# ScalarE one group ahead, VectorE copying the turned nodes, and products a group sooner, at the end of a graph layer

## The chip, the cores and the metric

The kernel runs on 1 core of one Trainium2 chip. The metric is the device time of a whole execution in microseconds. The engines are TensorE (PE, with its weight loads as PEld), VectorE (DVE), ScalarE (ACT), GpSimd (POOL) and SyncE (SP), each with its own instruction stream; they meet at semaphores. Everything is float32 where this case is concerned.

## What is computed

A graph of 6250 nodes with 128 features and 206250 edges goes through three graph convolutions, a layer norm, one attention layer and another layer norm. The change lies in the convolutions:

```
def _conv(x, row, col, edge_type, edge_weight, W, b):
    deg_inv_sqrt = jnp.where(deg > 0, deg ** (-0.5), 0)
    norm = deg_inv_sqrt[row] * deg_inv_sqrt[col] * edge_weight
    xw = jnp.einsum('ni,tio->tno', x, W)          # four edge types
    x_j = xw[edge_type, col] * norm[:, None]
    out = jax.ops.segment_sum(x_j, row, num_segments=N) + b
    return jax.nn.leaky_relu(out, negative_slope=0.01)
z1 = _conv(x, row, col, edge_type, edge_attr, W1, b1)
z2 = _conv(z1, row, col, edge_type, edge_attr, W2, b2)
z3 = _conv(z2, row, col, edge_type, edge_attr, W3, b3)
return (x + z1 + z2 + z3) / 4
```

## The kernel before

**Sizes.** Nodes are held as 49 blocks of 128 (`NB`), one node to a partition. The edges have been sorted by the block of their target row beforehand, into 1612 tiles of 128 edges. For each layer a table in memory (`gcn_table`) holds, for every node, its four products with the layer's four weight matrices, scaled by the node's `inv_deg`.

**A layer.** POOL issues one indirect transfer per tile (L718), which gathers the 128 table rows of the tile's edges into a ring of 93 tiles, `g_rows`. The other engines walk over 465 *groups* of four steps (`GRP`, `GP = 4`). A step is one tile and one target block; where a block begins inside a tile, the tile is used by two steps. In a group q:
- ACT (`scale_rows`, `scale`, L866 to L877) loads five registers from the list `gcn_at` (four ring slots and the last tile, L866), waits until the tile has landed (`s_land`) and copies four tiles with each edge's weight as scale to `g_step` (L877), a ring of three groups.
- DVE (`layer_gcn`) has built `g_hot` two groups before (L1579), four one-hot matrices in a ring of three.
- PE (`sum_gcn`, `add_up`, L1169 to L1180) loads four registers from `gcn_at`, zeroes a bank with one product (L1175) and adds four products of `g_hot` and `g_step` (L1180; each is two passes in the trace, so eight).
- DVE adds the bank to `acc` (L1588).

The first groups are in a hardware loop; the last ones are written out, with no loop.

**The end of a layer.** The first of the 49 blocks is sure to be complete at group 451 (`DONE_FROM`), and four more at each of the next 12 groups (`BATCHES`: one block, then twelve batches of four; `NBATCH = 13`). n is the batch, so group 451 + n. Of layers 0 and 1 each batch makes four blocks of the next layer's table:
- `next_z` on DVE (L1604, L1606, L1608): z of the batch, three instructions one after another, in the group n itself, behind the add to `acc`; then `s_z` is raised.
- `turn` on PE (L1141): four transposes of z into bank 4. In before they are put in group n + 1, as its last work.
- `turn` on ACT (L839): the copy of bank 4 to `nodeT`. It is a single buffer.
- `products` on PE (L1149): four products, nodeT of a block by the layer's 128x512 weights, into three banks in turn, so the fourth waits until the rows of the first are out. In before they are put in group n + 2, between the sums and the transposes.
- `rows_of` on ACT (L846): four copies to `rows` with `inv_deg` as scale, as the products come; SP writes each to the table (L492), through a ring of four.

So in before ACT's stream in group 451 + n is: registers, scale the group's own four tiles, rows of batch n - 2, copy of the turned batch n - 1. Before group 464 stand the rest: products 11, turn 12, products 12. POOL begins the next layer's gathers when all 49 table writes have landed and all of the layer's `g_rows` have been scaled (`s_copied`, all 465 groups).

Order is set by the code alone, since every engine's stream is written out by hand with its waits.

## Time and profile before

| | us |
|---|---|
| time before, median of 3 runs | 9099.33 (9099.24 to 9101.07) |
| the profiled execution's own time | 9109.24 |
| its span, first to last instruction | 9107.4 |
| PE busy | 5676.2 (62%) |
| DVE busy | 4601.6 (51%) |
| ACT busy | 3980.5 (44%) |
| POOL busy | 6423.1 (71%) |

The profiled execution is 9.9 us longer than the median. The busy shares are means over stages with different limits: sorting up to about 700 us, three layers up to about 6937 us, then attention. A line such as L718 is one source line of the kernel; "idle before" is what the engine stood still ahead of a group of instructions, and the arrow names what released it.

### The profile page before, as it was taken

What the parts mean: (1) busy time and instruction counts of PE and PEld (TensorE: products, weight loads), DVE (VectorE), ACT (ScalarE), POOL (GpSimd) and SP (SyncE); (2) the same over time, 40 slices, a digit from 0 to 9 for tenths busy, and PEclk for the clock granted to TensorE, in tenths of its full rate; (3) what the DMA queues carried; (4) which work ended last, traced back from release to release, by engine and by line L of the source; (5) the groups of instructions that cost most, each with busy time, mean ns of one, the idle gap of its engine ahead of it and who ended that gap; (6) DMA issues with size and microseconds to landing.
All of it is one profiled execution on the core that took longest, in us unless ns stands there. A gap on an engine that the chain in (4) does not pass through costs nothing.

```text
span 9107.4 us, 149340 instructions
## 1 busy us (share of the span) xinstructions
PE 5676.2 (62%) x32763; PEld 4294.9 (47%) x32764; DVE 4601.6 (51%) x12830; ACT 3980.5 (44%) x12251; POOL 6423.1 (71%) x6527
## 2 busy tenths in 40 slices
PE   4885555555555555555556555555654777777775
PEld 3664444444443444444443444444443666666665
DVE  9994232323233232322323232232325999999998
ACT  5552232323233232322323232232324888888887
POOL 0566777777775777777775777777775777777775
PEclk9996555555556555555556555555555787777876
DMA  1001111111123111111112111111111434343333
GB/s 50 32 35 54 53 53 53 53 53 53 53 67 79 53 53 53 53 53 53 53 53 90 53 53 53 53 53 53 53 53 57 117 114 116 115 115 115 115 115 94
DMA packets 432675, 612.43 MB, mean 67 GB/s; under 512 B 232026, under 2 KB 249479, under 8 KB 432527
## 3 DMA queue, kind: packets, MB, share of 16 engines
q0 software_dynamic: 208832, 428.96, 16.9%
q1 hardware_dynamic: 223694, 182.02, 6.3%
q14 instruction: 121, 0.98, 0.0%
q8 instruction: 28, 0.46, 0.0%
HBM read 437.29 MB, written 51.28 MB: 54 GB/s over the span
## 4 chain that ended last, share of the span: by engine, by line
issue 26%; POOL 25%; DMA 23%; DVE 18%; DVEq 4%; PE 4%; ACT 1%; POOLq 0%; ACTq 0%; SPq 0%
POOL g_rows L718 24%; DMA g_rows<-gcn_table,rec_idx 22%; DVEq L1563 3%; DVE a_miss L1674 2%; DVE a_max L1679 1%; DVE state L1732 1%; DVE lo_hot L1249 1%; DVE a_lo L1758 1%; DVE acc L1738 1%; DVE v_hot L1389 1%; PE wide L1149 1%; DVE a_sum L1702 1%; DVE state L1692 1%; DVE a_drop L1720 1%; DVE a_left L1753 1%
## 5 line engine op out<-in xcount | busy, mean ns | idle before, releaser
L718 POOL DMA_INDIRECT g_rows<-gcn_table,rec_idx x4836 | 4592.4, 950 | 1644.4 <-issue 1212.7
L877 ACT ACTIVATE g_step<-g_rows,rec_w 128x128 f32 x5580 | 1781.3, 389 | 4211.5 <-POOLq L698 3921.5
L1180 PE MATMUL bank<-g_step,g_hot 128*128 128x128 f32 x7440 | 1853.4, 428 | 1646.8 <-ACT g_step L877 1533.0
L1180 PEld LDWEIGHTS bank<-g_step,g_hot 128*128 128x128 f32 x7440 | 1593.5, 316 | 2078.9 <-issue 2078.9
L1588 DVE TENSOR_TENSOR acc<-acc,bank 128x512 f32 x930 | 639.9, 688 | 2765.4 <-PE bank L1180 2761.5
L743 POOL DMA_INDIRECT a_roll<-gat_table,src_plane x1612 | 1527.0, 947 | 494.4 <-issue 444.9
L1180 PE MATMUL wide<-g_step,g_hot 128*128 128x128 f32 x3720 | 930.0, 429 | 896.9 <-ACT g_step L877 871.0
L1180 PEld LDWEIGHTS wide<-g_step,g_hot 128*128 128x128 f32 x3720 | 799.8, 317 | 1111.7 <-issue 1111.7
L930 ACT ACTIVATE a_cand<-a_miss,a_rows 128x128 f32<-128x128 bf16 x3608 | 1096.0, 386 | 19.7 <-DMA a_rows<-a_roll 19.5
L1588 DVE TENSOR_TENSOR acc<-acc,wide 128x512 f32 x465 | 320.0, 688 | 1495.8 <-PE wide L1180 1494.1
L1579 DVE TENSOR_TENSOR g_hot<-bank,rec_lo 128x512 f32<-128x512 f32 x1395 | 952.7, 683 | 3.6 <-DVE z L1608 0.3
L1209 PE MATMUL bank<-a_msg,a_hot 128*128 128x130 f32 x3608 | 668.3, 341 | 384.8 <-DVE a_msg L1725 381.3
L1209 PEld LDWEIGHTS bank<-a_msg,a_hot 128*128 128x128 f32 x3608 | 566.7, 238 | 522.1 <-DVE a_msg L1725 402.3
L1200 PE MATMUL wide<-ident,a_cand 128*128 128x128 f32 x3608 | 689.1, 354 | 165.4 <-ACT a_cand L930 164.2
L1200 PEld LDWEIGHTS wide<-ident,a_cand 128*128 128x128 f32 x3608 | 551.8, 183 | 193.3 <-ACT a_cand L930 161.7
L580 POOL DMA_INDIRECT gcn_slots<-run,at_u x52 | 286.0, 5500 | 408.7 <-issue 399.0
L1679 DVE TENSOR_REDUCE a_max<-wide 128x2 f32<-128x1024 f32 x451 | 550.1, 1220 | 38.9 <-issue 24.9
L1175 PE MATMUL bank<-zeros 1*128 1x512 bf16 x930 | 537.1, 578 | 25.1 <-issue 8.1
L923 ACT ACTIVATE a_hot<-a_miss 128x512 f32<-128x512 bf16 x451 | 283.9, 629 | 255.2 <-DVE a_miss L1674 253.2
L1674 DVE TENSOR_TENSOR a_miss<-bank,a_lo 128x256 bf16<-128x256 f32 x902 | 375.8, 417 | 6.8 <-issue 0.8
L1725 DVE SCALAR_TENSOR_TENSOR a_msg<-bank,a_rows 128x520 f32<-128x520 f32 x451 | 312.5, 693 | 1.8 <-ACT bank L942 1.8
L918 ACT ACTIVATE a_hotT<-wide 128x512 bf16<-128x512 f32 x451 | 269.1, 597 | 87.1 <-DVE a_max L1679 77.5
(262 smaller groups left out, 5070.9 us busy)
## 6 DMA issues: line engine op xcount, KB each, us to landing
a_rows<-a_roll SPq DMA_DIRECT2D x451, 264.0 KB
g_rows<-gcn_table,rec_idx POOLq DMA_INDIRECT x4836
gcn_table<-rows SPq DMA_DIRECT2D x147, 256.0 KB, 2.0
a_roll<-gat_table,src_plane POOLq DMA_INDIRECT x1612
e_dst<-by_dst_dst SPq DMA_DIRECT2D x451, 2.0 KB
gat_table<-acc SPq DMA_DIRECT2D x7, 462.0 KB
out_x<-xs SPq DMA_DIRECT2D x6, 448.0 KB
gcn_slots<-nothing SPq DMA_DIRECT2D x4, 468.0 KB, 5.7
```

The source lines that it names most:

```text
L718: pool.indirect_dma_start(out=g_rows[:, tile % RING, :], out_offset=None, in_=gcn_tables[layer % 2], in_offset=bass.IndirectOffsetOnAxis(a ...
L743: pool.indirect_dma_start(out=a_roll[:, g % ROLL, t, :], out_offset=None, in_=gat_table, in_offset=bass.IndirectOffsetOnAxis(ap=src_plane[ ...
L877: last = nc.scalar.activation(g_step[:, j, k, :].unsqueeze(1), g_rows[:, bass.ds(slots[k], 1), :], ACT.Copy, scale=rec_w[:, bass.ds(q.at(0 ...
L930: last = nc.scalar.activation(a_cand[:, w, h, t, :], a_miss[:, j, t, :], ACT.Identity, scale=-BIG, bias=a_rows[:, j, t, ROW - HEADS + h:RO ...
L1175: nc.tensor.matmul(sums_of(j)[:, :], zeros[0:1, 0:1].to_broadcast([1, P]), zeros[0:1, 0:1].to_broadcast([1, GP * D]), start=True, stop=False)
L1180: last = nc.tensor.matmul(sums_of(j)[:, bass.ds(places[k], D)], g_hot[:, j % 3, k, :], g_step[:, j % 3, k, :], start=False, stop=(k == GP ...
L1200: last = nc.tensor.transpose(wide[:, w, h, t, :], a_cand[:, w, h, t, :], ident[:, :])
L1209: last = nc.tensor.matmul(pv_ps(j), a_hot[:, j, t, :], a_msg[:, j, t, :], start=(t == 0), stop=(t == T - 1))
L1579: V.tensor_tensor(g_hot[:, j, :, :], spread(iota_ps.unsqueeze(1), [P, GP, P]), spread(lo.unsqueeze(2), [P, GP, P]), ALU.is_equal).then_inc ...
L1588: V.tensor_tensor(dst_ap, dst_ap, sums_of(j).rearrange("p (k d) -> p k d", k=GP), ALU.add).then_inc(s_gadd, 1)
L1674: return V.tensor_tensor(a_miss[:, h, ts, :], spread(iota_ps.unsqueeze(1), [P, 2, P]), spread(a_lo[:, h, ts].unsqueeze(2), [P, 2, P]), ALU ...
L1679: V.tensor_reduce(a_max[:, m, :], wide[:, m % 2, :, :, :].rearrange("p h t e -> p h (t e)"), AX.X, ALU.max).then_inc(sa["max"], 1)
```

## The change

In the groups 451 to 463 of layers 0 and 1:
- ACT scales the tiles of the *following* group (group 451 does its own and the next), ahead of the rows; the registers for the group after that are loaded behind those copies (`slots_of`, kept in `ahead`). The rows come one batch sooner by number: those of n - 1 in group 451 + n.
- PE does the transposes of batch n at the end of the group 451 + n itself, and the products of batch n - 1 behind the sums; the registers of the next group are loaded between the products and the transposes.
- The copy of bank 4 to `nodeT` is DVE's, behind the batch's three z instructions, with a wait for the transposes. ACT has no such copy left.
- Before group 464 only the products and rows of batch 12 stand.

```
--- before.py
+++ after.py
@@ -832,12 +832,7 @@
             act.wait_ge(s_count, 9)

             def scale_rows(layer):
-                def turn(n):
-
-                    act.wait_ge(s_tT, turns(layer + 1, n) + 1)
-                    width = len(BATCHES[n])
-                    nc.scalar.copy(nodeT[:, 0:width, :].rearrange("p b e -> p (b e)"), bank[4][:, 0:width * P]
-                                   ).then_inc(s_tc, 1)
+                ahead = []

                 def rows_of(n):
                     for b in BATCHES[n]:
@@ -850,23 +845,26 @@
                     if not q.live(0):
                         return
                     n = q.base - DONE_FROM if q.i is None and layer < 2 else -1
-                    if n == NBATCH:
-                        rows_of(n - 2)
-                        turn(n - 1)
+                    if n <= 0:
+                        scale(q, slots_of(q))
+                    if 0 <= n < NBATCH:
+                        following = Step(GRP, q.base + 1)
+                        scale(following, ahead.pop() if n else slots_of(following))
+                        if n + 1 < NBATCH:
+                            ahead.append(slots_of(Step(GRP, q.base + 2)))
+                    if n >= 1:
                         rows_of(n - 1)
-                    scale(q)
-                    if 0 <= n < NBATCH:
-                        if n >= 2:
-                            rows_of(n - 2)
-                        if n >= 1:
-                            turn(n - 1)
-
-                def scale(q):
-                    j = q.slot(0) % 3
-                    _, (*found, tile) = nc.values_load_multi_w_load_instructions(
+
+                def slots_of(q):
+                    _, values = nc.values_load_multi_w_load_instructions(
                         gcn_at[32:33, bass.ds(q.at(0), 1), :].rearrange("p g k -> p (g k)"),
                         engines=(mybir.EngineType.Activation,), min_val=0, max_val=CH * CCOLS - 1,
                         skip_runtime_bounds_check_because="a step less the begun blocks, at most the last tile")
+                    return values
+
+                def scale(q, values):
+                    j = q.slot(0) % 3
+                    *found, tile = values
                     slots = [nc.s_assert_within(v, 0, RING - 1,
                                                 skip_runtime_bounds_check_because="a tile modulo the ring")
                              for v in found]
@@ -1132,6 +1130,8 @@
                     last.then_inc(s_flip, 1)

             def sum_gcn(layer):
+                ahead = []
+
                 def turn(n):

                     pe.wait_ge(s_z[layer + 1], BATCHES[n].stop)
@@ -1154,22 +1154,23 @@
                         return
                     n = q.base - DONE_FROM if q.i is None and layer < 2 else -1
                     if n == NBATCH:
-                        products(n - 2)
-                        turn(n - 1)
                         products(n - 1)
-                    add_up(q)
+                    add_up(q, ahead.pop() if n >= 1 else places_of(q))
                     if 0 <= n < NBATCH:
-                        if n >= 2:
-                            products(n - 2)
                         if n >= 1:
-                            turn(n - 1)
-
-                def add_up(q):
-                    j = q.slot(0)
+                            products(n - 1)
+                        ahead.append(places_of(Step(GRP, q.base + 1)))
+                        turn(n)
+
+                def places_of(q):
                     _, places = nc.values_load_multi_w_load_instructions(
                         gcn_at[64:65, bass.ds(q.at(0), 1), 0:GP].rearrange("p g k -> p (g k)"),
                         engines=(mybir.EngineType.PE,), min_val=0, max_val=(GP - 1) * D,
                         skip_runtime_bounds_check_because="a block less its group's first, at most one per step")
+                    return places
+
+                def add_up(q, places):
+                    j = q.slot(0)
                     if q.live(-3) or layer:
                         pe.wait_ge(s_gadd, q.at(-3, 1, ADDS * layer + 2))
                     nc.tensor.matmul(sums_of(j)[:, :], zeros[0:1, 0:1].to_broadcast([1, P]),
@@ -1591,6 +1592,11 @@
                         if 0 <= n < NBATCH:
                             dve.wait_ge(s_gadd, q.at(0, 1, adds + 2))
                             next_z(layer, slice(BATCHES[n].start, BATCHES[n].stop))
+                            if layer < 2:
+                                dve.wait_ge(s_tT, turns(layer + 1, n) + 1)
+                                width = len(BATCHES[n])
+                                V.tensor_copy(nodeT[:, 0:width, :].rearrange("p b e -> p (b e)"),
+                                              bank[4][:, 0:width * P]).then_inc(s_tc, 1)
                 run_steps(dve, GRP, 3, 2, body, NBATCH + 1)
                 dve.wait_ge(s_gadd, adds + ADDS)
```

PE's stream, one group of the written-out end of layer 0 (group 458, batch 7). L1149 are the products, L1141 the transposes, L1175 (in after L1176) the zeroing, L1180 (L1181) the sums. Before:

```order
L1149 MATMUL wide<-w_all,nodeT 128x512 [waits s_tr,s_tc]
L1149 MATMUL wide<-w_all,nodeT 128x512 [waits s_tr]
L1149 MATMUL bank<-w_all,nodeT 128x512 [waits s_tr]
L1149 MATMUL wide<-w_all,nodeT 128x512 [waits s_tr]
L1141 MATMUL wide<-ident,z 128x128 [waits s_tc,s_z1]
L1141 MATMUL wide<-ident,z 128x128 x3
L1169 TENSOR_LOAD gcn_at
L1175 MATMUL wide<-zeros 128x512 [waits s_gadd]
L1180 ISA [waits s_copied,s_ghot]
L1180 MATMUL wide<-g_step,g_hot 128x128
```

And after:

```order
L1149 MATMUL wide<-w_all,nodeT 128x512 [waits s_tr,s_tc]
L1149 MATMUL bank<-w_all,nodeT 128x512 [waits s_tr]
L1149 MATMUL wide<-w_all,nodeT 128x512 [waits s_tr] x2
L1166 TENSOR_LOAD gcn_at
L1141 MATMUL wide<-ident,z 128x128 [waits s_tc,s_z1]
L1141 MATMUL wide<-ident,z 128x128 x3
L1176 MATMUL wide<-zeros 128x512 [waits s_gadd]
L1181 ISA [waits s_copied,s_ghot]
L1181 MATMUL wide<-g_step,g_hot 128x128
```

The kinds of work stand in the same row, but the register load moved ahead of the transposes, and by the numbers of the batches the transposes are now those of the group's own batch, and the products those of the batch before it.

ACT's stream at the same place, from the scaling of one group to the next. L877 (in after L875) is one tile's scaling, L846 (L841) one block's rows, L839 the copy to nodeT, and the TENSOR_LOAD the five registers. Before:

```order
L866 TENSOR_LOAD gcn_at
L875 REGISTER_ALU [waits s_gpe]
L877 ISA [waits s_land]
L877 ACTIVATE g_step<-g_rows,rec_w 128x128
...
L846 ACTIVATE rows<-wide,inv_deg 128x512 [waits s_tw1,s_tm]
L846 ACTIVATE rows<-wide,inv_deg 128x512 [waits s_tw2,s_tm]
L846 ACTIVATE rows<-bank,inv_deg 128x512 [waits s_tw3,s_tm]
L846 ACTIVATE rows<-wide,inv_deg 128x512 [waits s_tw0,s_tm]
L839 COPY nodeT<-wide 128x512 [waits s_tT]
```

And after:

```order
L873 REGISTER_ALU [waits s_gpe]
L875 ISA [waits s_land]
L875 ACTIVATE g_step<-g_rows,rec_w 128x128
...
L859 TENSOR_LOAD gcn_at
L841 ACTIVATE rows<-wide,inv_deg 128x512 [waits s_tw1,s_tm]
L841 ACTIVATE rows<-wide,inv_deg 128x512 [waits s_tw2,s_tm]
L841 ACTIVATE rows<-bank,inv_deg 128x512 [waits s_tw3,s_tm]
L841 ACTIVATE rows<-wide,inv_deg 128x512 [waits s_tw0,s_tm]
```

The copy L839 left the stream, and the register load went from ahead of the scaling to behind it.

DVE's stream at the same place, in after, where L1589 is the add to acc, L1610 to L1614 the three z instructions and L1580 the one-hots of the group after next:

```order
L1589 TENSOR_TENSOR acc<-acc,wide 128x4x128
L1610 TENSOR_TENSOR z<-acc,inv_deg 128x512 [waits s_gadd]
L1612 TENSOR_TENSOR z<-z,bias 128x512 [waits s_chain]
L1614 SCALAR_TENSOR_TENSOR z<-z 128x512 [waits s_chain]
L1598 COPY nodeT<-wide 128x512 [waits s_chain,s_tT]
L1580 TENSOR_TENSOR g_hot<-bank,rec_lo 128x512 [waits s_gpe]
```

L1598 is the copy that came from ACT; before, the one-hots followed z at once.

## Rows read from the trace of the kernel before

**Rows 1.** Page: a group's instructions, busy us, mean ns, idle before it
```profile
L718 POOL DMA_INDIRECT g_rows<-gcn_table,rec_idx x4836 | 4592.4, 950 | 1644.4 <-issue 1212.7
```
**Rows 2.** Timeline of POOL at the boundaries: start us, us, and idle before
```profile
2736.13 1.15 POOL L718 DMA_INDIRECT g_rows<-gcn_table,rec_idx  x1 [0.30 <-issue]
2812.79 0.94 POOL L718 DMA_INDIRECT g_rows<-gcn_table,rec_idx  x1 [75.52 <-DMA gcn_table<-rows]
...
4911.65 0.94 POOL L718 DMA_INDIRECT g_rows<-gcn_table,rec_idx  x1 [77.64 <-DMA gcn_table<-rows]
```
**Rows 3.** Chain that ended last, the group from 2781 us: start, us, what
```profile
2782.78 1.15 PE bank L1180 x8
2783.93 1.52 PE bank L1149 x2
2785.45 2.76 PE wide L1149 x4
2788.20 0.87 PE bank L1149 x2
2789.10 0.69 ACT rows L846
2789.79 0.48 ACTq L866
2790.26 1.13 issue
```
**Rows 4.** Timeline of DVE, PE and ACT, a z hand-over, then the same group
```profile
2706.89 0.69 DVE L1608 SCALAR_TENSOR_TENSOR z<-z 128x512 f32<-128x512 f32 x1
...
2707.93 0.14 PEld L1141 LDWEIGHTS wide<-ident,z 128*128 128x128 f32 x1 [0.24 <-DVEq L1611]
...
2781.26 1.28 ACT L877 ACTIVATE g_step<-g_rows,rec_w 128x128 f32 x4 [1.31 <-issue]
...
2784.08 0.69 DVE L1588 TENSOR_TENSOR acc<-acc,bank 128x512 f32 x1 [6.61 <-PE bank L1180]
...
2786.25 0.69 DVE L1608 SCALAR_TENSOR_TENSOR z<-z 128x512 f32<-128x512 f32 x1
...
2788.47 0.14 PEld L1141 LDWEIGHTS wide<-ident,z 128*128 128x128 f32 x1 [0.24 <-issue]
...
2789.43 0.38 PE L1175 MATMUL bank<-zeros 1*128 1x512 bf16 x1
2789.69 0.58 ACT L839 COPY nodeT<-wide 128x512 f32<-128x512 f32 x1
2791.56 1.28 ACT L877 ACTIVATE g_step<-g_rows,rec_w 128x128 f32 x4 [1.30 <-issue]
```
**Rows 5.** Timeline, the last batch's products (before group 464)
```profile
2805.60 0.30 PEld L1149 LDWEIGHTS bank<-w_all,nodeT 128*128 128x128 f32 x2 [1.06 <-ACT nodeT L839]
...
2809.23 0.09 PEld L1175 LDWEIGHTS wide<-zeros 1*128 1x128 bf16 x1 [0.76 <-issue]
...
2809.34 0.69 ACT L846 ACTIVATE rows<-bank,inv_deg 128x512 f32<-128x512 f32 x1 [0.17 <-PE bank L1149]
```
**Rows 6.** Groups of DVE by form: a copy from PSUM, busy us, mean ns
```profile
L1470 DVE COPY start_row<-bank 128x200 f32<-128x200 f32 x1 | 0.4, 366 | 0.0
```
**Rows 7.** Timeline, sums of groups 452 and 453, and the second boundary's 452
```profile
2690.54 2.07 PE L1180 MATMUL wide<-g_step,g_hot 128*128 128x128 f32 x8 [3.58 <-ACT g_step L877]
...
2695.71 2.07 PE L1180 MATMUL bank<-g_step,g_hot 128*128 128x128 f32 x8 [2.36 <-ACT g_step L877]
...
4788.12 2.07 PE L1180 MATMUL wide<-g_step,g_hot 128*128 128x128 f32 x8 [2.35 <-DVE g_hot L1579]
```
**Rows 8.** Windows: stretch, us, busy (x) of PE, PEld, DVE, ACT, POOL, granted clock, DMA
```profile
2779.60:2782.70 3.10, 0.00 (x0) 0.00 (x0) 0.00 (x0) 1.63 (x5) 0.00 (x0) 1.00 0.42 155
...
2784.30:2787.50 3.20, 3.20 (x5) 1.33 (x4) 2.54 (x4) 0.99 (x2) 0.00 (x0) 0.51 0.15 56
2787.50:2790.00 2.50, 2.32 (x9) 0.97 (x7) 0.00 (x0) 1.97 (x4) 0.00 (x0) 1.00 0.45 170
```

## The prediction

> **What bounds the kernel now.** I read the page first: POOL's gathers are the longest group, 4836 of them at 950 ns, idle before them by 0.30 us each for "issue" [rows 1]. One gather follows the other every 1.25 us, 1612 times per layer, and nothing in the change touches that. Then POOL's own timeline, to see where it stands still: after the last gather of a layer it waits 75.52 us at the first boundary and 77.64 us at the second, both times for the table writes [rows 2]. These 153 us are all that the change can shorten, and as POOL is last on both sides of the wait, every microsecond less there is one less in the end. The gathers of layer 0 are over at 2736.12 + 1.15 = 2737.3 us, a floor far below 2812.8.
>
> The chain of waits tells what fills the stretch. From one group to the next it goes round once: sums on PE (1.15), four products (1.52 + 2.76 + 0.87 = 5.15), the last rows on ACT (0.69), the register load (0.48 + 1.13 = 1.61), the scaling of the next group, then the sums again [rows 3]. The scaling of one group begins at 2781.26 and that of the next at 2791.56 [rows 4]: once round takes 10.3 us. PE, ACT and the register load work in turn, and no engine is full.
>
> **What the change does to the loop.** It cuts the one loop into several that run side by side. I call S the end of a group's sums (2783.93 in [rows 3]) and work out when S of the next group can be.
>
> *Through DVE and the transposes.* The add to acc begins at S + 0.15, z ends at 2786.25 + 0.69, that is S + 3.01 [rows 4]. Where the transposes waited for z, they loaded at 2707.93, 0.35 after z's end at 2707.58 [rows 4], so here the transposes load at S + 3.36. From that load to the zeroing are 0.96 (2788.47 to 2789.43), the zeroing takes 0.38 [rows 4], the sums 1.15 [rows 3]: next S at S + 5.85.
>
> *Through the products on PE.* They are queued ahead of the transposes. With nothing in their way they take, from their first weight load to the next other instruction, with a register load between the two, 2809.23 - 2805.60 = 3.63 [rows 5]. They begin at S, so the transposes can load at S + 3.63, and the next S is at 6.12. This holds at the higher clock.
>
> *Through ACT.* Four rows follow the products at the pace of the products: from the first row's start to the last one's 2.6 (three products of 0.87 [rows 3]), then 0.69, the scaling 1.28 [rows 4], and the register load of 1.61 if all of it lies open, since it now stands behind the scaling and ahead of the rows: 6.18, and with a tenth for the hand-over between them, assumed, 6.3. If half of it runs under the scaling, this loop is shorter than the other two.
>
> *Through DVE alone.* ACT's copy began 1.22 after the transposes' load (2788.47 to 2789.69 [rows 4]), and I let DVE's do the same. Its length on DVE has no row; ACT's takes 0.58 [rows 4], a DVE copy from PSUM of 200 columns takes 0.366 [rows 6], and at about 1 ns per further column, 512 give 0.68, which is also what DVE's other 512-column work takes. I take 0.68 (bounds 0.58 and 0.9). With the one-hots of 0.69 behind it, DVE is free 2.6 after the transposes' load, and the next sums are there at 2.65. It is just hidden. Its new wait holds up the one-hots (two groups ahead of need, so nobody waits) and the next add.
>
> The slowest of these is ACT's, so I take **6.3 us a group**, with 5.85 as the lower bound and 7.3 as the upper, which adds 1.0 for one more open register load or a stretch at the lower clock. Of the register load the Trainium skill says, in DMA: Bandwidth & Descriptors, Latency and other measured facts, that a tensor_load has a floor of about 600 ns; this trace shows 1.61 for five registers [rows 3]. By 0.6 ACT's loop would be 5.3, PE's 6.12 would bind, and the sum would be 9024; the trace has the word.
>
> **The sum.** At the first boundary S of group 452 is 2690.54 + 2.07 = 2692.61, and it waits for gathered tiles, so it stays [rows 7]. Before, group 453 ended at 2697.78. Now its sums stand behind the transposes of batch 1: z at +3.36 gives 2695.97, and at the lower clock transposes and zeroing take twice as long and the sums 2.07: 1.92 + 0.76 + 2.07, so 2700.7; *this group is 2.9 later than before*. For group 454 I take 7.0 (partly at the lower clock): 2707.7. Nine more at 6.3: 2764.4 for S of group 463. Then z and the transposes' load (3.36), the copy (1.22 + 0.68), 0.35 to PE, products until the last rows start 3.74 (2805.60 to 2809.34 [rows 5]), rows 0.69, and 2.76 from the end of the last rows (2810.03) to POOL's start (2812.79 [rows 2]): together 12.8. POOL resumes at 2777.2 in place of 2812.79: **35.6 us less**. The second boundary: S of 452 is 4790.19 [rows 7], POOL resumes 121.46 later; now 84.6: 36.9 less. Both: 72.5.
>
> Nothing follows at once to eat it. The next layer's first sums wait for gathers in both kernels. The z instructions and the copies now fall closer together among a layer's last gathers, and some of those may grow, as the last one with 1.15 in place of 0.95 [rows 1, 2]. At a third of a microsecond for each of five more batches that is 2 us, on gathers that end by 2740; POOL resumes 37 us after that. The floor is not reached.
>
> The profiled execution would go from 9109.24 to 9037, and the median of the runs, 9.9 below it, from 9099.33 to 9026.8, rounded to **9027**. With 5.85 in the nine groups it is 9027 - 2 x 9 x 0.45 = 9019, and with early groups at the higher clock (2.5 less each time) 9014; with 7.3, 9045.
>
> **Rivals.**
> *The loops don't run side by side cleanly.* Three engines load registers in the middle of their work, the fourth product waits for ACT's first rows, and those stand behind a scaling and a load. Each late row makes the products late, the transposes behind them, and the next sums. For it speaks that the first three paths differ by 0.4 only. Against it, the load on PE is in the 3.63 already. It gives 7.3 to 8.8 a group: 18 groups by 1.0 to 2.5 more, 9045 to 9072.
> *PE at half clock.* The granted clock is 0.51, the lower of the two levels (1.2 GHz), in the 3.2 us that follow an idle stretch of 3.1, and 1.00 behind them [rows 8]. All products at the lower clock would be twice four of 0.87, that is 7.0; with the 1.92, 0.76 and 2.07 from above a group takes 11.8. Ten groups from 2700.7, then 12.8 and another 3.5 for the last products, put POOL's start at 2835, 22 later than before, and 20 at the second boundary: 9099 + 42 = 9141, slower than before. It decides from 9.9 a group upward (2812.79 - 12.8 - 2700.7, by ten). Against it: PE would be busy 5.9 of 6.3 us, and the drop comes behind 3 us without any work on PE, which no longer occur. The Trainium skill tells the same of the clock in TensorE: Matmul & The Clock Gate, Part 1: half rate is what it starts from, and full rate comes after sustained work. By that rule too the new loop is the warm one unless it gets gaps.
> *Nothing gained.* If the table writes or the scaled tiles were last for another reason, for example if ACT's scaling of the following group waited for gathers late into the end, rows would queue behind it. The gathers arrive at 1.25 us a tile, 1612 tiles to 465 groups, 4.3 us a group, faster than 6.3; only the first groups can wait. It would give 9085 to 9115.
>
> **How the numbers follow.** The forecast (5.85 to 7.2 a group, 9012 to 9045) gets 0.72, the unclean loops 0.17, nothing gained 0.05, the lower clock 0.06. Within 0.2% (18 us, about what a measurement of this kernel can tell) lies the third alone: same 0.05, slower 0.06, faster 0.89. The range reaches from 9012, a little below the lower bound, to 9066 in the second case; outside lie 0.05 + 0.06 and some 0.06 of the second case.
>
> **What would show it.** POOL's wait for the table writes at 38 to 42 us instead of 75.5 and 77.6, and its gathers unchanged at 1.25. Scaling to scaling 6.3 in the last ten groups, with granted clock near 1.0 from group 455 on. DVE's copy at 0.68, and its add right behind the sums. Rows of a batch 0.86 apart. Group 453's sums ending near 2700.7. The prediction is wrong if POOL's wait stays above 60, if PE has gaps above 1 us per group, or if the gathers grow longer elsewhere.

## The result and the profile after

The changed kernel takes **9004.5 us** (median of 4 runs, 9002.9 to 9005.5) where the kernel before, on the same chip, takes 9099.3: a ratio of 0.9895, 95% interval 0.9878 to 0.9912. It is faster by 94.8 us. The direction was predicted; the forecast of 9027 was 22.5 too high, and the time lies 7.5 under the lower end of the range. The profiled execution took 9004.9 (span 9003.1) beside 9109.2 of before.

POOL's timeline at the two layer boundaries, which answers to [rows 2] (start us, us, idle before in brackets):

```profile
2735.00 0.94 POOL L718 DMA_INDIRECT g_rows<-gcn_table,rec_idx  x1 [0.30 <-issue]
...
2763.39 6.20 POOL L718 DMA_INDIRECT g_rows<-gcn_table,rec_idx  x1 [27.45 <-DMA gcn_table<-rows]
...
4809.91 6.77 POOL L718 DMA_INDIRECT g_rows<-gcn_table,rec_idx  x1 [26.57 <-DMA gcn_table<-rows]
```

The waits fall from 75.52 and 77.64 to 27.45 and 26.57; I had expected 38 to 42. The rest of the gathers are as they were (page, answers to [rows 1]):

```profile
L718 POOL DMA_INDIRECT g_rows<-gcn_table,rec_idx x4836 | 4587.4, 949 | 1545.4 <-issue 1219.9
```

Their busy time differs by 5.0 us in 4592. Of the idle time ahead of them, 1644.4 before, 99.0 are gone, and the two waits are 99.1 shorter.

One group of the changed loop, the timeline of DVE, PE and ACT, from the sums of one group to those of the next:

```profile
2734.41 1.26 ACT L875 ACTIVATE g_step<-g_rows,rec_w 128x128 f32 x4
2734.46 1.16 PE L1181 MATMUL bank<-g_step,g_hot 128*128 128x128 f32 x8
2734.86 0.68 DVE L1580 TENSOR_TENSOR g_hot<-bank,rec_lo 128x512 f32<-128x512 f32 x1
2735.35 0.30 PEld L1149 LDWEIGHTS wide<-w_all,nodeT 128*128 128x128 f32 x2
...
2735.76 0.69 DVE L1589 TENSOR_TENSOR acc<-acc,bank 128x512 f32 x1 [0.22 <-PE bank L1181]
...
2736.52 0.69 ACT L841 ACTIVATE rows<-wide,inv_deg 128x512 f32<-128x512 f32 x1 [0.84 <-PE wide L1149]
...
2737.94 0.69 DVE L1614 SCALAR_TENSOR_TENSOR z<-z 128x512 f32<-128x512 f32 x1
...
2738.74 0.51 PEld L1141 LDWEIGHTS wide<-ident,z 128*128 128x128 f32 x4 [0.52 <-DVEq L1617]
...
2739.09 0.69 ACT L841 ACTIVATE rows<-wide,inv_deg 128x512 f32<-128x512 f32 x1 [0.17 <-PE wide L1149]
2739.42 0.09 PEld L1176 LDWEIGHTS wide<-zeros 1*128 1x128 bf16 x1 [0.17 <-issue]
...
2739.53 0.69 DVE L1598 COPY nodeT<-wide 128x512 f32<-128x512 f32 x1 [0.90 <-PE wide L1141]
2739.68 1.26 ACT L875 ACTIVATE g_step<-g_rows,rec_w 128x128 f32 x4
2739.74 1.16 PE L1181 MATMUL wide<-g_step,g_hot 128*128 128x128 f32 x8
```

Sums to sums (2734.46 to 2739.74) and scaling to scaling take **5.28 us**, against 10.3 before and 6.3 in the forecast. ACT, which I had named as the bound, scales as soon as its last rows are out (no idle time in the row at 2739.68) and then stands still for 0.84, waiting for products. So its register load doesn't lie open. DVE waits 0.22 and 0.90 a group. Rows of the windows view (stretch, us, then busy time and count of PE, PEld, DVE, ACT, POOL, granted clock, DMA) say who is full; the last one holds five whole groups, from sums to sums:

```profile
2689.00:2698.00 9.00, 7.22 (x25) 5.01 (x26) 5.33 (x9) 3.24 (x9) 6.87 (x8) 0.69 0.25 75
2698.00:2713.00 15.00, 15.00 (x57) 7.85 (x56) 10.62 (x17) 10.95 (x22) 11.65 (x12) 0.98 0.64 215
...
2723.00:2757.00 34.00, 33.22 (x133) 18.42 (x133) 24.41 (x36) 24.25 (x50) 10.01 (x10) 1.00 0.65 230
...
2723.90:2750.30 26.40, 26.40 (x107) 14.61 (x106) 20.27 (x31) 19.57 (x42) 9.30 (x10) 1.00 0.66 230
```

In those five groups PE has no idle time at all, at a granted clock of 1.00, and it reaches that clock one or two groups earlier than I let it. A part of the gain is the clock: from the first product to the transposes PE takes 3.44 us at this clock, where the four products took 5.15 before, with the granted clock at 0.51 for a part of them [rows 3, 8].

### The profile page after: what moved, and what is told of

It is laid out like the page before. It is cut to its first block, busy times and chain, and to the rows that moved or that the text cites. A ratio compares the mean times of both kernels' runs of the same rounds, so it can differ in the third digit from the quotient of the medians.

```text
span 9003.1 us, 149340 instructions
## 1 busy us (share of the span) xinstructions
PE 5648.8 (63%) x32763; PEld 4282.5 (48%) x32764; DVE 4616.6 (51%) x12856; ACT 3964.5 (44%) x12225; POOL 6419.3 (71%) x6527
## 4 chain that ended last, share of the span: by engine, by line
issue 26%; POOL 25%; DMA 22%; DVE 18%; DVEq 4%; PE 3%; ACT 1%; POOLq 0%; ACTq 0%; SPq 0%
POOL g_rows L718 25%; DMA g_rows<-gcn_table,rec_idx 22%; DVEq L1564 3%; DVE a_miss L1680 2%; DVE a_max L1685 1%; DVE state L1738 1%; DVE lo_hot L1250 1%; DVE acc L1744 1%; DVE a_lo L1764 1%; DVE v_hot L1390 1%; DVE a_sum L1708 1%; DVE state L1698 1%; DVE a_drop L1726 1%; DVE a_left L1759 1%; DVE a_part L1753 1%
## 5 line engine op out<-in xcount | busy, mean ns | idle before, releaser
L875 ACT ACTIVATE g_step<-g_rows,rec_w 128x128 f32 x5580 | 1781.4, 389 | 4200.3 <-POOLq L698 3896.2
L1181 PE MATMUL bank<-g_step,g_hot 128*128 128x128 f32 x7440 | 1851.9, 427 | 1601.8 <-ACT g_step L875 1494.4
L1181 PEld LDWEIGHTS bank<-g_step,g_hot 128*128 128x128 f32 x7440 | 1592.7, 316 | 2032.9 <-issue 2032.9
L1589 DVE TENSOR_TENSOR acc<-acc,bank 128x512 f32 x930 | 639.5, 688 | 2691.6 <-PE bank L1181 2686.5
L1181 PE MATMUL wide<-g_step,g_hot 128*128 128x128 f32 x3720 | 928.0, 428 | 860.9 <-ACT g_step L875 833.1
L1181 PEld LDWEIGHTS wide<-g_step,g_hot 128*128 128x128 f32 x3720 | 798.0, 317 | 1076.3 <-issue 1076.3
L1589 DVE TENSOR_TENSOR acc<-acc,wide 128x512 f32 x465 | 319.8, 688 | 1427.8 <-PE wide L1181 1426.2
L1580 DVE TENSOR_TENSOR g_hot<-bank,rec_lo 128x512 f32<-128x512 f32 x1395 | 952.5, 683 | 0.4
L1176 PE MATMUL bank<-zeros 1*128 1x512 bf16 x930 | 536.8, 577 | 25.6 <-issue 9.3
```

What stands on the lines that cost most here:

```text
L875: last = nc.scalar.activation(g_step[:, j, k, :].unsqueeze(1), g_rows[:, bass.ds(slots[k], 1), :], ACT.Copy, scale=rec_w[:, bass.ds(q.at(0 ...
L1176: nc.tensor.matmul(sums_of(j)[:, :], zeros[0:1, 0:1].to_broadcast([1, P]), zeros[0:1, 0:1].to_broadcast([1, GP * D]), start=True, stop=False)
L1181: last = nc.tensor.matmul(sums_of(j)[:, bass.ds(places[k], D)], g_hot[:, j % 3, k, :], g_step[:, j % 3, k, :], start=False, stop=(k == GP ...
L1580: V.tensor_tensor(g_hot[:, j, :, :], spread(iota_ps.unsqueeze(1), [P, GP, P]), spread(lo.unsqueeze(2), [P, GP, P]), ALU.is_equal).then_inc ...
L1589: V.tensor_tensor(dst_ap, dst_ap, sums_of(j).rearrange("p (k d) -> p k d", k=GP), ALU.add).then_inc(s_gadd, 1)
```

## The experiments

The place of the gain was predicted and its size was not, so the question is what sets the 5.28 us. **Theory A**: PE's own stream of work and the way through DVE's z are equally long and bind together; ACT's and DVE's parts and the register loads are covered. **Theory B**: one thing alone binds, ACT's loop with its load (my forecast) or z. The comparison is always with the kernel before, measured beside each variant on the same chip (its median lay at 9098.8 to 9099.3); where I set two variants side by side, I use their medians (the changed kernel's is 9004.5). The letters in an expectation are those that it explains itself.

### Which part carries the gain

*The copy back on ScalarE.* All as changed, but ACT copies the turned nodes, right ahead of its rows:

```diff
                     if n >= 1:
                         rows_of(n - 1)
+                    if 0 <= n < NBATCH:
+                        act.wait_ge(s_tT, turns(layer + 1, n) + 1)
+                        width = len(BATCHES[n])
+                        nc.scalar.copy(nodeT[:, 0:width, :].rearrange("p b e -> p (b e)"),
+                                       bank[4][:, 0:width * P]).then_inc(s_tc, 1)
...
-                            if layer < 2:
-                                dve.wait_ge(s_tT, turns(layer + 1, n) + 1)
-                                width = len(BATCHES[n])
-                                V.tensor_copy(nodeT[:, 0:width, :].rearrange("p b e -> p (b e)"),
-                                              bank[4][:, 0:width * P]).then_inc(s_tc, 1)
```

> The changed kernel, but ScalarE copies the turned nodes again, behind the rows of its group. Theory A (a group of 5.28 us is set by VectorE's add and three z instructions, the transposes, the zeroing and the sums; ScalarE has slack, 0.85 us of waiting before its first rows): the copy of 0.58 us goes into the slack, 5.3 to 5.5 us a group, 9003 to 9012 us. Theory B, that of my prediction (ScalarE's own loop is the slowest): 0.6 us more in each of 24 groups, 9019 us or more.

Measured: 9003.2 us (9003.1 to 9004.0), ratio 0.9895 (0.9878 to 0.9911), POOL's waits 27.2 and 27.0, the last five groups again 5.28 apart. The move of the copy from ACT to VectorE brings nothing. In the changed kernel ACT has 0.84 us of idle time a group, and the copy (0.58 there) goes into it: 0.37 to 0.62 of idle time are left.

*Only the scaling ahead.* The kernel before, with ACT scaling the following group and loading the registers for it a group earlier; the copy, the order on PE and the products stay (`scale` is parted into `slots_of` and `scale` as in the change):

```diff
-                    scale(q)
+                    if n <= 0:
+                        scale(q, slots_of(q))
                     if 0 <= n < NBATCH:
+                        following = Step(GRP, q.base + 1)
+                        scale(following, ahead.pop() if n else slots_of(following))
+                        if n + 1 < NBATCH:
+                            ahead.append(slots_of(Step(GRP, q.base + 2)))
                         if n >= 2:
                             rows_of(n - 2)
...
```

> The kernel before with one part of the change: ScalarE scales one group ahead with registers loaded ahead; its copy of the turned nodes, the place of the transposes and of the products stay as before. Theory A: PE's own stream is then the bound, with its register load open (0.5): about 5.8 us a group, and the end of the layer has one more batch to turn and multiply, 5 us: 9099 less 2 x 39, about 9025 us. If products sooner or VectorE's copy carry the gain: above 9060 us.

Measured: 9012.1 us (9008.2 to 9014.6), ratio 0.9903 (0.9886 to 0.9920), POOL's waits 35.7 and 31.2. Some 87 of the 95 us come with this part alone. I had expected 9025 and 5.8 a group: here too the last six groups are 5.28 apart, as PE's timeline shows, with DVE's add waiting 1.57 us for the sums, so that z isn't late in this kernel:

```profile
2730.91 0.09 PEld L1186 LDWEIGHTS bank<-zeros 1*128 1x128 bf16 x1 [0.17 <-issue]
...
2732.53 0.69 DVE L1599 TENSOR_TENSOR acc<-acc,bank 128x512 f32 x1 [1.57 <-PE bank L1191]
...
2736.19 0.09 PEld L1186 LDWEIGHTS bank<-zeros 1*128 1x128 bf16 x1 [0.17 <-issue]
```

PE's register load stands between the transposes and the zeroing in this kernel, and it isn't open: the zeroing's weight load follows with 0.17 of "issue".

The other 8 us are in the ends. In this kernel, as before, two batches are still to be multiplied when the last group comes, in the changed one it is one: from the sums of group 463 to those of 464 are 14.75 us at both boundaries (2752.34 to 2767.09 at the first), against 9.76 in the changed kernel (2750.30 to 2760.06), 5.0 each time. The early groups give some of it back, 3.0 at the first boundary and 2.1 at the second (from the sums of 452 to those of 454 are 10.0 at the first, against 13.1), and one group at the first boundary takes 9.11 (sums 2705.69 to 2714.80). There ACT's scaling of the following group waits for its tiles, the rows stand behind it, and PE's fourth product waits for the rows:

```profile
2709.71 1.28 ACT L888 ACTIVATE g_step<-g_rows,rec_w 128x128 f32 x4 [3.65 <-POOLq L698]
...
2711.27 0.69 ACT L848 ACTIVATE rows<-wide,inv_deg 128x512 f32<-128x512 f32 x1 [0.28 <-issue]
...
2712.01 1.47 PE L1160 MATMUL wide<-w_all,nodeT 128*128 128x512 f32 x2 [2.59 <-ACT rows L848]
```

(L698 is POOL's signal that tiles have landed.) This is the mechanism of my third rival, in one group. The rest of the change (products, transposes and PE's register load sooner, the copy on DVE) is worth these 8 us once the scaling is ahead.

*All but the scaling ahead.* The changed kernel, with ACT scaling the group's own tiles ahead of the rows, its registers loaded a group earlier:

```diff
-                    if n <= 0:
-                        scale(q, slots_of(q))
+                    if n == NBATCH:
+                        rows_of(n - 1)
+                    scale(q, ahead.pop() if n >= 1 else slots_of(q))
                     if 0 <= n < NBATCH:
-                        following = Step(GRP, q.base + 1)
-                        scale(following, ahead.pop() if n else slots_of(following))
-                        if n + 1 < NBATCH:
-                            ahead.append(slots_of(Step(GRP, q.base + 2)))
-                    if n >= 1:
-                        rows_of(n - 1)
+                        ahead.append(slots_of(Step(GRP, q.base + 1)))
+                        if n >= 1:
+                            rows_of(n - 1)
```

> The changed kernel, but ScalarE scales the rows of its own group again, with the registers still loaded ahead; products sooner and VectorE's copy stay. Both theories: scaling (1.28) and sums (1.15) now follow the last rows, which start 3.5 us behind the sums: 6.9 us a group in place of 5.28, 22 groups by 1.6, about 9040 us. If the scaling of the own group were hidden anyway: 9005 us.

Measured: 9031.4 us (9029.7 to 9037.5), ratio 0.9925 (0.9908 to 0.9942), POOL's waits 41.0 and 43.6. The timeline of ACT and PE:

```profile
2729.51 1.27 ACT L873 ACTIVATE g_step<-g_rows,rec_w 128x128 f32 x4
...
2731.02 1.16 PE L1179 MATMUL wide<-g_step,g_hot 128*128 128x128 f32 x8 [1.39 <-ACT g_step L873]
...
2733.08 0.69 ACT L841 ACTIVATE rows<-bank,inv_deg 128x512 f32<-128x512 f32 x1 [2.30 <-PE bank L1147]
...
2736.24 1.27 ACT L873 ACTIVATE g_step<-g_rows,rec_w 128x128 f32 x4
```

Now PE waits 1.39 for ACT and ACT 2.30 for PE, one after the other, and a group takes 6.73 (2729.51 to 2736.24), not the 6.9 that I expected; my 9040 counted 22 such groups. This is a loop through both engines: scaling, sums, first products, rows. Its removal needs the scaling of the *following* group, and 27 us hang on that.

The parts don't add up: the scaling ahead alone brings 87 us, everything else without it 67, both together 95. Either one opens the loop of 10.3. The run without the scaling ahead still has ACT's registers loaded ahead, and no run separates that from the products sooner.

### What sets 5.28

*One instruction more in z.* A fourth DVE instruction of the same size, which changes no value:

```diff
                 if layer < 2:
+                    chain(V.scalar_tensor_tensor(z[:, bs, :], z[:, bs, :], 1.0, z[:, bs, :],
+                                                 ALU.mult, ALU.max))
```

> The changed kernel with one more instruction on z in every batch of layers 0 and 1 (it multiplies by one and changes nothing), 0.72 us. Theory A: all of it on the path, 24 batches, 9005 + 17 = 9022 us. Theory B (ScalarE's loop is the slowest): some of it hidden, 9005 to 9012 us.

Measured: 9019.0 us (9015.8 to 9020.2), ratio 0.9911 (0.9894 to 0.9927), POOL's waits 36.7 and 33.2. The transposes' weight load now waits longer for DVE, and sums are mostly 5.91 apart (2703.53, 2709.45, 2715.36) where they were 5.28:

```profile
2731.44 0.69 DVE L1617 SCALAR_TENSOR_TENSOR z<-z 128x512 f32<-128x512 f32 x1
...
2732.24 0.66 PE L1141 MATMUL wide<-ident,z 128*128 128x128 f32 x4 [0.42 <-DVEq L1619]
```

The instruction adds 0.72 from start to start (2730.71 to 2731.44), and 0.63 of it come out. So z's path has a slack of 0.09, no more: in this run it binds at 5.91, and without the added instruction it would be 5.19. The time is 14.5 us over the changed kernel; 18 groups by 0.63 and one instruction of 0.69 at each end are 12.7 of them, and the runs of this variant spread over 4.4.

*One instruction less in z.* The bias is not added in layers 0 and 1:

```diff
-                chain(V.tensor_tensor(z[:, bs, :], z[:, bs, :],
-                                      spread(bias[:, layer, :].unsqueeze(1), shape), ALU.add))
+                if layer == 2:
+                    chain(V.tensor_tensor(z[:, bs, :], z[:, bs, :],
+                                          spread(bias[:, layer, :].unsqueeze(1), shape), ALU.add))
```

> The changed kernel with one DVE instruction less in z: the adding of the bias is left out in layers 0 and 1, so the numbers computed are others. Repeated for the same reason. Theory A (z's path and PE's own stream are nearly equal; PE alone needs about 5.0 us a group): the period goes from 5.28 to 5.0, 18 groups by 0.28 plus 0.6 at each end, 8998. Theory B (z alone binds, by 5 us a group or more): the whole 0.63 shows, 18 by 0.63 plus the ends, 8992.

Measured: 9003.4 us (9002.3 to 9004.6), ratio 0.9895 (0.9879 to 0.9912): 1.1 us under the changed kernel, within the spread. Both numbers that I had written down were wrong. The timeline of DVE and PE tells why:

```profile
2737.65 0.19 PEld L1149 LDWEIGHTS wide<-w_all,nodeT 128*128 128x128 f32 x1 [0.24 <-issue]
...
2738.24 0.62 PEld L1141 LDWEIGHTS wide<-ident,z 128*128 128x128 f32 x4 [0.40 <-issue]
2738.51 0.60 PE L1141 MATMUL wide<-ident,z 128*128 128x128 f32 x4
...
2739.14 0.69 DVE L1598 COPY nodeT<-wide 128x512 f32<-128x512 f32 x1 [1.62 <-PE wide L1141]
...
2739.35 1.16 PE L1181 MATMUL wide<-g_step,g_hot 128*128 128x128 f32 x8
```

DVE is now idle for 1.62 us ahead of its copy, the transposes no longer wait for z ("issue" in place of DVE), and yet the sums begin at 2734.08, 2739.35, 2744.63, 5.28 apart. PE's own stream is 5.28 long, not 5.0 as I had estimated: from the start of the sums to the start of the products 0.99, products 3.44, transposes 0.53, zeroing 0.31. So PE's stream binds, and z's path of 5.19 stands 0.09 behind it. Theory A holds nearly: the two are not equal, but so close that of what is added to z all but 0.09 a group comes out, and what is taken from it brings nothing.

### What the register loads cost

*ACT's load late.* The changed kernel, ACT loading right before the scaling:

```diff
-                        scale(following, ahead.pop() if n else slots_of(following))
-                        if n + 1 < NBATCH:
-                            ahead.append(slots_of(Step(GRP, q.base + 2)))
+                        scale(following, slots_of(following))
```

> The changed kernel, but ACT loads the registers of the following group's scaling right before it, behind the waits, and not a group earlier. Repeated, since the first run of it was on a chip where the kernel before took 12050 us. Theory A (the load runs beside work; PE and the z path bind at 5.3 us a group, ACT has 0.85 us of idle time a group): at most the part of 1.6 us that exceeds 0.85 comes out, 18 groups by 0 to 0.75, 9005 to 9017. Theory B (the load was on the path all the time, as the prediction had it): +1.6 a group, 9034 to 9040.

Measured: 9010.7 us (9008.4 to 9014.1), ratio 0.9902 (0.9886 to 0.9919), POOL's waits 30.3 and 32.0; 6.2 us over the changed kernel. The scaling now does stand behind an idle stretch on ACT:

```profile
2743.65 1.28 ACT L873 ACTIVATE g_step<-g_rows,rec_w 128x128 f32 x4 [1.77 <-PE wide L1179]
```

Seven of the ten scalings from 2703.77 to 2753.78 stand behind 1.38 to 2.17 us of idle time, and 0.3 a group come out in the end (sums 2702.35 to 2753.53, nine groups of 5.69, against 5.37 in the changed kernel). ACT's 0.84 of idle time takes a part of it. Another part comes back because the products are ready by then, in three banks: ACT starts rows 0.57 apart (2744.83, 2745.40) where it had to wait for each product, 0.86 apart, in the changed kernel. Theory A.

*PE's load late*, behind the transposes and not ahead of them:

```diff
-                    add_up(q, ahead.pop() if n >= 1 else places_of(q))
+                    add_up(q, places_of(q))
...
-                        ahead.append(places_of(Step(GRP, q.base + 1)))
```

> The changed kernel, but PE loads the registers of a group's sums right ahead of them, behind the transposes, and not ahead of the transposes. Repeated for the same reason. Theory A (PE's stream and z bind together, the load of 0.6 to 1.1 us now stands between the transposes and the zeroing): +0.5 to 0.9 a group, 18 groups, 9013 to 9021. Theory B (the wait for DVE's z hides PE's load wherever it stands): 9005.

Measured: 9018.9 us (9014.8 to 9020.3), ratio 0.9911 (0.9894 to 0.9927), POOL's waits 35.5 and 36.1; 14.4 us over the changed kernel. The zeroing behind the transposes now comes late in most groups, and not in every one:

```profile
2737.18 0.39 PE L1175 MATMUL bank<-zeros 1*128 1x512 bf16 x1
...
2743.40 0.37 PE L1175 MATMUL wide<-zeros 1*128 1x512 bf16 x1 [0.88 <-issue]
```

On PE, which is full, an open load costs nearly all that it lasts: 0.81 to 1.15 us in seven of the nine groups from 2707.70 to 2755.85, and the period rises from 5.37 to 6.04 (sums 2701.77 to 2756.15). On ACT, which has idle time, it costs about a fifth of its length. But the place alone doesn't open the load: in the kernel with only the scaling ahead it is the same one, PE is as full (31.67 of 31.67 us busy in its last six groups), and nothing comes out. What differs is that there the transposes are those of the batch before, whose z is long done, while here they wait for z (until 2741.77), and the load comes behind that wait. That this is the reason is my reading; no run varies it alone, and it leaves open why two groups of nine go free.

The two late variants, the one with less z and the next one had each a first run on a chip where the kernel before took 12050 us. They took 11966.5 (ACT's load late), 11969.6 (PE's), 11959.0 (less z) and 11949.4 us (the next one), 83, 80, 91 and 100 less than it. DVE and ACT wait there for up to 24 us at a time for what the profile calls "remote", and I draw nothing from these runs.

### A version that is faster than both

At each boundary a gather takes 6.2 to 7.4 us instead of 0.94. In the kernel before it is the third one after the wait, in the changed kernel the first, and DVE's update of the layer's input begins 1.2 us ahead of it (1.3 in the changed kernel), at the first boundary. The timeline of DVE and POOL in the kernel before, and then in the changed one:

```profile
2814.08 6.69 DVE L1598 SCALAR_TENSOR_TENSOR xs<-xs,z 128x6272 f32<-128x6272 f32 x1
2815.28 6.31 POOL L718 DMA_INDIRECT g_rows<-gcn_table,rec_idx  x1 [0.31 <-issue]
```

```profile
2762.09 6.69 DVE L1604 SCALAR_TENSOR_TENSOR xs<-xs,z 128x6272 f32<-128x6272 f32 x1
...
2770.23 5.61 DVE L1571 MEMSET acc<- 128x6656 f32 x1 [1.45 <-issue]
2771.14 0.94 POOL L718 DMA_INDIRECT g_rows<-gcn_table,rec_idx  x1 [0.30 <-issue]
```

The gather at 2763.39 ends at 2769.59, 0.81 behind the end of that instruction. The same holds at both boundaries in the kernels before and after and in the seven variants above: the long gather begins 0.07 to 2.60 behind the instruction's start, takes 7.44 to 4.91 accordingly, and always ends 0.81 to 0.83 behind its end. I moved the instruction ahead of the last group's add, where DVE stands idle (5.31 us in the changed kernel) and POOL still waits:

```diff
+                        if layer < 2 and q.i is None and q.base == DONE_FROM + NBATCH:
+                            chain(V.scalar_tensor_tensor(xs[:, :, :], xs[:, :, :], 1.0 if layer else 5.0,
+                                                         z[:, :, :], ALU.mult, ALU.add))
...
-                if layer < 2:
-                    chain(V.scalar_tensor_tensor(xs[:, :, :], xs[:, :, :], 1.0 if layer else 5.0, z[:, :, :],
-                                                 ALU.mult, ALU.add))
```

> The changed kernel with DVE's update of the layer's input (one instruction over 128 x 6272, 6.7 us) moved from behind the last add to ahead of it, where DVE waits for the sums of the last group. Repeated for the same reason. Theory A (that instruction holds up POOL's first gather, 6.2 us long, at both boundaries): the gather falls to about 1 us and 2 x 5.2 us go, 8994. Theory B (the gather is long for its table's first read or the clock of something else): 9004. If the instruction is still running when the last add could begin, some of it comes back as a longer tail, at most 2 us each time.

Measured: **8994.0 us** (8993.2 to 8994.9), ratio 0.9884 (0.9868 to 0.9901), 10.5 less than the changed kernel:

```profile
2755.13 6.68 DVE L1587 SCALAR_TENSOR_TENSOR xs<-xs,z 128x6272 f32<-128x6272 f32 x1
...
2761.95 0.69 DVE L1592 TENSOR_TENSOR acc<-acc,wide 128x512 f32 x1
2762.50 0.94 POOL L718 DMA_INDIRECT g_rows<-gcn_table,rec_idx  x1 [27.40 <-DMA gcn_table<-rows]
...
4804.70 0.94 POOL L718 DMA_INDIRECT g_rows<-gcn_table,rec_idx  x1 [27.41 <-DMA gcn_table<-rows]
```

Both gathers are 0.94, and no gather of the whole execution is longer than 1.5. The last add begins 0.6 later, at 2761.95, and POOL's wait for the table hardly changes by it (27.45 and 26.57, now 27.40 and 27.41). Theory A of this run, to within a microsecond.

## Why the prediction was right in direction and wrong in size

**Where the time is.** Right. All of it is in the two waits of POOL: 48.1 and 51.1 us less of them. Nothing else gave it back.

**Which step failed.** The period of 6.3 a group, measured 5.28, and in it two terms. ACT's 1.61 of register load, laid open in the loop, was covered; but without it the forecast's own next bound was 6.12, so this is worth 0.18 of the 1.02. The other 0.84 are the products' path on PE, the one that binds: 6.12 forecast, 5.28 measured. The lower bound of 5.85 was too long in the same way, and with it the range.

**The early groups.** Mis-sized. S of group 452 comes at 2691.01, and S of 453 at 2696.94; I had 2700.7, *later* than before. S of 452, which I had held fixed, is 1.6 earlier. The granted clock rises already in the next group:

```profile
2688.93 2.08 PE L1181 MATMUL wide<-g_step,g_hot 128*128 128x128 f32 x8
...
2694.13 0.66 PE L1141 MATMUL wide<-ident,z 128*128 128x128 f32 x4 [1.78 <-DVEq L1617]
...
2695.04 1.90 PE L1181 MATMUL bank<-g_step,g_hot 128*128 128x128 f32 x8
...
2701.98 1.16 PE L1181 MATMUL bank<-g_step,g_hot 128*128 128x128 f32 x8
```

The group takes 5.93 and not 8.1, the next 6.2 and not 7.0: 3.0 us less than my sum.

**The path through DVE and the transposes, 5.85.** Its rows add up to 5.28 in the changed kernel, 0.09 of which is waiting for PE. The add at S + 0.14 and the end of z at S + 3.01 were right to 0.01. The hand-over to PE takes 0.11 (z ends at 2738.63, the load begins at 2738.74), not 0.35; from there to the zeroing 0.68, not 0.96, since that figure was read where the load had to queue behind products; the zeroing holds up the sums 0.32, not its length of 0.38. That is 0.24 + 0.28 + 0.06. With no product in front, as in the run with more z (2732.24 to 2732.83), the 0.68 are 0.59, and the path is 5.19.

**The path through the products, 6.12.** It was 5.28, and it binds. The products don't begin at S but 0.28 ahead of it (load 2734.96, S 2735.24 in the run with less z), since the modelled end of the sums overlaps them. From their load to the transposes' are 3.28, not 3.63. I had counted PE's register load into the 3.63 of [rows 5], and wrongly. The changed kernel has the same stretch before group 464, with no register load in it (its registers were loaded a group earlier), and it is again 3.63 long, with the same 0.76 of "issue":

```profile
2756.11 1.12 PE L1149 MATMUL bank<-w_all,nodeT 128*128 128x512 f32 x2 [0.78 <-DVE nodeT L1598]
...
2759.74 0.09 PEld L1176 LDWEIGHTS wide<-zeros 1*128 1x128 bf16 x1 [0.76 <-issue]
```

What differs is that the transposes' weight load starts under the last product, 0.27 ahead of the transposes (2738.24 and 2738.51), and the zeroing's doesn't. From there the transposes take 0.80, and not 0.96, and the zeroing 0.31. I had added the lengths of instructions that PE overlaps; what counts is start to start.

**The path through ACT, 6.3.** I laid 1.61 us of register load open in the loop, though it stands behind a scaling of 1.26 and ahead of a wait for products, and I had myself written that it might run under the scaling. Scaling and wait cover it: ACT's row of 2736.52 waits for PE, not for "issue". What is left of ACT's path, 3.1 of rows and 1.3 of scaling, leaves the 0.84 idle. The bound that I named was the shortest of the three: 4.4, beside 5.19 and 5.28.

**DVE's copy.** 0.69, as forecast (0.68), beginning 0.79 after the transposes' load and not 1.22. Its cover held, and the time would be the same with the copy on ACT.

**The sum.** From S of 452 to POOL's start, predicted 84.6 twice, measured 72.4 and 71.8 (S of layer 1's 452 at 4738.09). The first 12.2 come from: group 453 2.2, group 454 0.8, nine groups (48.3 instead of 56.7) 8.4, and the tail (11.93 instead of 12.8) 0.9. The nine groups average 5.37, as one of them took 6.05: DVE loads registers for its adds in every third group, and that time the load lay open, so that the add came 0.88 later behind the sums than in the others (2714.75, with 1.10 of "issue" before it); 0.77 came out, the rest is z's slack. At the second boundary the nine average 5.49. Predicted gain 72.5, measured by these terms 97.4; the medians differ by 94.8. The profiled executions differ by 104.4, and 6.9 of that lie outside the two stretches (1.6 ahead of the first, 2.7 between, 2.6 behind), less than the 9.9 by which the profiled execution of before lies above its median.

**The rivals.** Unclean loops (one group of 6.05 in nine), half clock (0.98 and more from 2698 on) and nothing gained did not come. What I had held against the first, that PE's register load was in the 3.63 already, was not so. The Trainium skill's figure, in DMA: Bandwidth & Descriptors, Latency and other measured facts, could not decide either way: with the load covered its length is not on the path, whether it is a floor of about 600 ns or the 1.61 of [rows 3]. It erred on the helpful side: by it ACT's loop came to 5.3, and 9024.

**The range** was too narrow at its lower end. I had bounded the period by one path (5.85) that was itself a sum of rows read in a loop with queues. A bound from below must leave out what a row holds of waiting and what PE overlaps.

## What to carry to other kernels

When a serial loop is cut into several, work out each new path from start to start, and take hand-overs from places where nothing was queued. Ask of each register load what stands around it on its engine: ahead of a wait it was free here; close behind a wait on the full engine it cost nearly what it lasts, and on an engine with idle time about a fifth. Before adding to an engine that shares a loop with another, see how far apart the two paths are: here, 0.09 us apart, an instruction less on the shorter one brought nothing, and one more cost nearly its full length. When a forecast takes the slowest of several paths, check the second slowest as closely, for it is the forecast as soon as the first one falls. And the part of an edit that carries the gain is found only by running the parts: here the scaling ahead alone brought 87 of 95 us, all the rest without it 67, the copy nothing.

## What the hardware showed beside that

A DVE instruction over 128 x 6272 with two operands in SBUF (6.69 us) holds up the gather that POOL issues beside it, to 6.20 and 6.77 us instead of 0.94, until 0.81 to 0.83 us behind its own end; moved away, the gathers are 0.94 again. A DVE memset over 128 x 6656 that writes only (5.61 us) leaves the gathers beside it at 0.94. Both were in the kernel before, unseen by me, because the long gather stood behind the wait that I was looking at.

The short z instructions do the same on their scale. At the end of layer 0 in the changed kernel, all eleven gathers that start while one of them runs (2692.16 to 2732.21) take 1.02 to 1.43 us, and each ends 0.81 to 0.83 behind that instruction, here at 2717.70 behind 2716.88. The thirteen that start beside DVE's one-hots, adds and copies, which read a bank, take 0.94 or 0.95:

```profile
2716.19 0.69 DVE L1612 TENSOR_TENSOR z<-z,bias 128x512 f32<-128x512 f32 x1
2716.29 1.41 POOL L718 DMA_INDIRECT g_rows<-gcn_table,rec_idx  x1 [0.30 <-issue]
```
